# Graph attention on one core: one edge column of every group fetched by one-hot products, in batches of three groups

## The reference

```python
nf = relu(layernorm(x)); ef = edge_attr
for l in range(3):
    f = leaky_relu((nf @ W_ni)[src] + (nf @ W_nj)[dst] + ef @ W_fij + bias, 0.2)
    e = einsum('ehd,hd->eh', f.reshape(-1, 4, 32), attn)
    a = softmax of e over the edges of one dst
    h = segment_sum((nf @ W_node)[src] * a, dst)
    nf, ef = h.mean(heads), f.mean(heads)
return x + nf
```

## Time and profile before

| | |
|---|---|
| median of 3 runs | 3000.43 us (3000.24 to 3002.9) |
| span of the profiled execution | 3006.7 us |
| mean granted PE clock | 0.843 of full speed |
| busy share of the span | DVE 83%, PE 80%, POOL 68%, PEld 62%, ACT 48% |

### The profile page before, as it was taken

How to read it: one execution, slowest core, us unless ns; L and a number is a source line. 1 busy time by engine, 2 the same in 40 slices (tenths; PEclk the granted TensorE clock), 3 DMA queues, 4 the chain that set the end, 5 groups by cost and what they waited for, 6 DMA issues and landing times.

```text
span 3006.7 us, 50077 instructions
## 1 busy us (share of the span) xinstructions
PE 2404.8 (80%) x15871; PEld 1878.0 (62%) x16027; DVE 2490.5 (83%) x6428; ACT 1447.6 (48%) x3416; POOL 2058.9 (68%) x2167
## 2 busy tenths in 40 slices
PE   3388888888887378888888887649999888998984
PEld 1366667676764356667766665337777777776753
DVE  7399999999997468998999998637888888879784
ACT  0155555555555135555556555414445454445452
POOL 6777777777770577777777776377776666667653
PEclk9699988888899589987999999857778787778796
DMA  6235454535342324343435342332333343333222
GB/s 252 64 96 156 122 147 116 152 110 158 110 128 85 112 74 142 119 149 110 157 111 158 110 153 98 118 103 67 100 120 99 98 136 98 108 108 100 91 92 81
DMA packets 139275, 353.92 MB, mean 118 GB/s; under 512 B 43895, under 2 KB 96027, under 8 KB 120207
## 3 DMA queue, kind: packets, MB, share of 16 engines
q1 hardware_dynamic: 67216, 296.09, 27.9%
q0 software_dynamic: 68960, 39.71, 8.6%
q10 hardware_dynamic: 2838, 14.91, 1.3%
HBM read 137.79 MB, written 212.77 MB: 117 GB/s over the span
## 4 chain that ended last, share of the span: by engine, by line
PE 39%; DVE 29%; issue 14%; ACT 9%; POOL 5%; DMA 3%; SPq 1%; DVEq 0%; ACTq 0%; POOLq 0%
DVE U L1349 12%; PE f_ps L695 12%; PE pick_ps L664 10%; PE f_ps L704 9%; PE xT_ps L685 5%; DVE rows L1266 4%; DVE lr L1277 4%; DVE U L1334 3%; POOL rows L554 2%; ACT f_low L850 2%; ACT xT L841 2%; ACT up L901 2%; PE f_ps L714 2%; ACT wide_ps L889 1%; DVE rows L1378 1%
## 5 line engine op out<-in xcount | busy, mean ns | idle before, releaser
L554 POOL DMA_INDIRECT rows<-nf_tab,src_sb x1995 | 1889.3, 947 | 706.9 <-issue 574.9
L704 PEld LDWEIGHTS f_ps<-w_out,lr 128*128 128x128 f32 x4836 | 701.0, 210 | 379.0 <-issue 277.3
L664 PE MATMUL pick_ps<-nf_part,z 125*128 125x160 bf16 x6345 | 630.0, 264 | 258.4 <-issue 217.0
L1349 DVE TENSOR_TENSOR_SCAN U<-wide_ps,U 128x272 f32<-128x272 f32 (+2 forms) x1272 | 801.6, 694 | 3.2 <-ACT wide_ps L889 2.4
L695 PE MATMUL f_ps<-xT,w_edge 97*128 97x512 f32 x1212 | 753.8, 708 | 22.6 <-ACT ef_new L872 12.0
L664 PEld LDWEIGHTS pick_ps<-nf_part,z 125*128 125x128 bf16 x6345 | 564.6, 112 | 289.8 <-issue 241.3
L704 PE MATMUL f_ps<-w_out,lr 128*128 128x36 f32 (+1 forms) x4836 | 649.8, 274 | 31.2 <-DVE lr L1277 28.8
L1277 DVE TENSOR_TENSOR lr<-f_ps,f_low 128x512 f32<-128x512 f32 x606 | 410.0, 677 | 252.4 <-ACT f_low L850 247.0
L850 ACT ACTIVATE f_low<-f_ps 128x512 f32<-128x512 f32 x606 | 361.0, 596 | 495.9 <-PE f_ps L695 495.9
L685 PE MATMUL xT_ps<-ident,rows 128*97 128x128 f32 x2418 | 431.8, 305 | 76.8 <-issue 37.2
L841 ACT ACTIVATE xT<-xT_ps 97x512 f32<-97x512 f32 x606 | 358.8, 592 | 147.8 <-PE xT_ps L685 145.6
(11 more groups left out here) (163 smaller groups left out, 1070.5 us busy)
## 6 DMA issues: line engine op xcount, KB each, us to landing
u_tab<-up SPq DMA_DIRECT2D x144, 1088.0 KB
s_nd<-edge_first SPq DMA_DIRECT2D x48, 768.0 KB
rows<-nf_tab,src_sb POOLq DMA_INDIRECT x1995, 2.5
ef_tab<-ef_new SPq DMA_DIRECT2D x32, 768.0 KB
ef_st<-ef_tab SPq DMA_DIRECT2D x32, 768.0 KB
z<-fifth_tab SPq DMA_DIRECT2D x141, 96.0 KB
edge_first<-s_nd ACTq DMA_DIRECT2D x16, 768.0 KB
ef_st<-in_edge_attr_dram SPq DMA_DIRECT2D x16, 672.0 KB
```

The source lines that it names most:

```text
L554: eng.indirect_dma_start(rows[q % RING][:, c * K:c * K + D], None, nf_tab[:, :], bass.IndirectOffsetOnAxis(ap=src_sb[:, t:t + 1], axis=0)) ...
L664: mm = eng.matmul(pick_ps[:, i * PB:(i + 1) * PB], hot[m % 2][0:NQ, f * PW + i * P:f * PW + (i + 1) * P], nf_part[a][0:NQ, f * PB:(f + 1) ...
L704: mm = eng.matmul(f_ps[n % 2][:, u * m:(u + 1) * m], lr[y][:, u * P:(u + 1) * P], w_out[l][:, 0:m], start=True, stop=True)
L1349: last = eng.tensor_tensor_scan(uh[:, c0 * w:c1 * w], dbc[h % 2][:, 0:(c1 - c0) * w], uh[:, c0 * w:c1 * w], 0.0, ALU.mult, ALU.add)
```

## The change

Every group now has a picked column (groups 0 to 182 of a layer, 61 batches instead of 47), and a batch is three consecutive groups, not three out of four. PE picks in every iteration g up to 173, column i = g % 3 of batch g // 3 + 3, where it ran a filling in every fourth; the fillings stay in iterations 174 to 181. Three batches are picked ahead of the loop, where it was two. DVE's `pick_rows` comes with g % 3 equal to 2 and `make_hot` with g % 3 equal to 0. The first write of `pick_rows` moves to ACT (`take_picks`, at the end of ACT's iteration), and so does the copy of the carry (`carry`, after `take_scores`, ahead of `lay_out`). The two subtractions of `soften` become one instruction over both halves of joined buffers, and `weigh` waits for that one and no longer for the addition behind it. SP loads the index rows by a running count.

```diff
-    NPICK = END // GB + 1
+    NPICK = END // PICK
+    AHEAD = 3
...
         def picks(g):
-            return g % GB < PICK and g // GB < NPICK
+            return g < PICK * NPICK
...
+                    loaded = IDXB + 4
+                    for b in range(IDXB + 2, loaded):
+                        load_fifths(l, b)
...
-                            if b + IDXB + 2 < NPICK:
-                                load_fifths(l, b + IDXB + 2)
+                            while loaded < min(4 * b // PICK + 10, NPICK):
+                                load_fifths(l, loaded)
+                                loaded += 1
...
-                    for b in range(2):
+                    for b in range(AHEAD):
                         for i in range(PICK):
                             pick(b, i)
...
                         turn(g + 2)
-                        b, i = g // GB + 2, g % GB
-                        if g >= 0 and i < PICK and b < NPICK:
+                        b, i = g // PICK + AHEAD, g % PICK
+                        if g >= 0 and b < NPICK:
                             pick(b, i)
                         elif g >= 1:
                             warm(g + 1, FILL_STEADY)
...
                     def weigh(k):
-                        eng.wait_ge(expo_done, k * 3 + 3)
+                        eng.wait_ge(expo_done, k * 2 + 1)
...
+                    def carry(k):
+                        w, before = sub_w(k % NB), sub_w(k % NB - 1)
+                        eng.wait_ge(sums_done, H * k)
+                        eng.activation(carry_of(U[k % 2], w)[:, :, 0, :],
+                                       carry_of(U[1 - k % 2], before)[:, :, before, :],
+                                       ACT.Copy).then_inc(carried, 1)
+
+                    def take_picks(b):
+                        m = l * NPICK + b
+                        q = l * NS + b * PICK // GS
+                        eng.wait_ge(pick_ready, PICK * (m + 1))
+                        if q >= RING:
+                            eng.wait_ge(turned, groups_to(q - RING))
+                            eng.wait_ge(prod_done, subs_to(q - RING))
+                        eng.activation(picked_rows(l, b), pick4[:, :, 0, :], ACT.Copy
+                                       ).then_inc(picked, 1)
...
                         if i == 1 and g >= 2 * GB:
+                            carry(k)
                             lay_out(k - 1)
+                        if g >= 0 and g % PICK == PICK - 1 and g // PICK + AHEAD < NPICK:
+                            take_picks(g // PICK + AHEAD)
...
-                        eng.tensor_tensor(ed3[:, :, 1:w + 1], mx3[:, :, 0:w],
-                                          mx3[:, :, 1:w + 1], ALU.subtract
-                                          ).then_inc(expo_done, 1)
-                        eng.tensor_tensor(e_wt[s][:, 0:w * H].rearrange("p (h t) -> p h t", h=H),
-                                          sc3[:, :, 1:w + 1],
-                                          mx3[:, :, 1:w + 1], ALU.subtract
-                                          ).then_inc(expo_done, 1)
+                        both = [P, 2, H, w]
+                        eng.tensor_tensor(
...
+                            ALU.subtract).then_inc(expo_done, 1)
...
-                            eng.tensor_copy(u4[:, :, 0, :], carry_of(U[1 - s], before)[:, :, before, :]
-                                            ).then_inc(carried, 1)
...
                     def pick_rows(b):
-                        eng.wait_ge(pick_ready, PICK * (m + 1))
...
-                        eng.tensor_copy(to, pick4[:, :, 0, :]).then_inc(picked, 1)
                         for v in range(1, PARTS5):
...
-                        if g >= 0 and i == PICK - 1 and b + 3 < NPICK:
-                            pick_rows(b + 3)
-                        if g >= 0 and i == 0 and b + 4 < NPICK:
-                            make_hot(b + 4)
+                        m = g // PICK + AHEAD
+                        if g >= 0 and g % PICK == PICK - 1 and m < NPICK:
+                            pick_rows(m)
+                        if g >= 0 and g % PICK == 0 and m + 1 < NPICK:
+                            make_hot(m + 1)
```

More of the change, by code:

```diff
@@ L135, in egat_kernel @@
         U = [sb(f"U{s}", [P, CH * W1]) for s in range(2)]
-        mx = [sb(f"mx{s}", [P, H * W1]) for s in range(2)]
+        HW1 = H * W1
+        mx_sc = [sb(f"mx_sc{s}", [P, 2 * HW1 + 2]) for s in range(2)]
+        mx = [a[:, 0:HW1] for a in mx_sc]
+        sc = [a[:, HW1:2 * HW1] for a in mx_sc]
         up = [sb(f"up{s}", [P, SB * UR]) for s in range(2)]
         up3 = [a[:, :].rearrange("p (t c) -> p t c", c=UR) for a in up]
-        sc = [sb(f"sc{s}", [P, H * W1]) for s in range(2)]
-        e_dec = [sb(f"e_dec{s}", [P, H * W1]) for s in range(2)]
-        e_wt = [sb(f"e_wt{s}", [P, H * SB]) for s in range(2)]
+        e_dw = [sb(f"e_dw{s}", [P, 2 * HW1]) for s in range(2)]
+        e_dec = [a[:, 0:HW1] for a in e_dw]
+        e_wt = [a[:, HW1:2 * HW1] for a in e_dw]
         xT = [sb(f"xT{s}", [P, GT * P]) for s in range(2)]
@@ L351, in rows_sem_to, with picked_rows @@
                             if (v % NS) * GS + a < NG)
+        def picked_rows(l, b):
+            s, c = divmod(b * PICK * GT + 2, SUP)
+            return rows3[(l * NS + s) % RING][:, c:c + GT * (PICK - 1) + 1:GT, 0:D]
         def carry_of(u, w):
@@ L678, in turn @@
                         if picks(g):
-                            eng.wait_ge(picked, PARTS5 * (l * NPICK + g // GB + 1))
+                            eng.wait_ge(picked, PARTS5 * (l * NPICK + g // PICK + 1))
                         if n >= 2:
@@ L887, in widen @@
                             eng.wait_ge(sums_done, 4 * k + h - 1)
+                        if h == 0:
+                            eng.wait_ge(expo_done, k * 2 + 2)
                         w, n = sub_w(k % NB) + 1, C - D // 2
@@ L910, in _ @@
                     put_ef(0)
+                    for b in range(AHEAD):
+                        take_picks(b)
                     kl = l * NB - 1
@@ L1015, in _ @@
                     widen(k + 1, 0)
+                    carry(k + 1)
                     lay_out(k)
@@ L1303, in soften @@
                         eng.wait_ge(max_done, k + 1)
-                        eng.tensor_tensor(ed3[:, :, 1:w + 1], mx3[:, :, 0:w],
-                                          mx3[:, :, 1:w + 1], ALU.subtract
-                                          ).then_inc(expo_done, 1)
-                        eng.tensor_tensor(e_wt[s][:, 0:w * H].rearrange("p (h t) -> p h t", h=H),
-                                          sc3[:, :, 1:w + 1],
-                                          mx3[:, :, 1:w + 1], ALU.subtract
-                                          ).then_inc(expo_done, 1)
-                        eng.wait_ge(expo_done, 3 * k + 1)
+                        both = [P, 2, H, w]
+                        eng.tensor_tensor(
+                            e_dw[s][:, :].rearrange("p (a x) -> p a x", a=2)[:, :, 0:n]
+                            .rearrange("p a (h t) -> p a h t", h=H)[:, :, :, 1:w + 1],
+                            mx_sc[s][:, :].rearrange("p (a x) -> p a x", a=2)[:, :, 0:n]
+                            .rearrange("p a (h t) -> p a h t", h=H)[:, :, :, 0:w],
+                            wide(mx[s][:, 0:n].rearrange("p (o h t) -> p o h t", o=1, h=H)
+                                 [:, :, :, 1:w + 1], both),
+                            ALU.subtract).then_inc(expo_done, 1)
+                        eng.wait_ge(expo_done, 2 * k + 1)
                         eng.tensor_tensor(ed3[:, :, 1:w + 1], ed3[:, :, 1:w + 1],
@@ L1387, in _ @@
                     pick_rows(1)
+                    make_hot(3)
+                    pick_rows(2)
                     slice_b(0)
```

30 lines of the change are left out of this document (10 added, 20 removed).

## The result

| | before | after |
|---|---|---|
| median, runs alternating on one chip | 3001.66 us (4 runs) | 3843.66 us (4 runs, 3835.13 to 3868.38) |
| span of the profiled execution | 3006.7 us | 3839.6 us |
| mean granted PE clock | 0.843 | 0.762 |

The ratio is **1.279**, with an interval of 1.273 to 1.285: 842 us slower. The forecast was 700 us slower, 3700 us, and the range ended at 3830. Direction and mechanism came as forecast; the size lies 14 us beyond the range.

A forecast was written before the change was run, and what follows sets the result against it. DVE was taken to bound the kernel at full clock. Twelve groups: 49.1 + 1.3 work + 1.2 first write + 16.3 chains = 67.9 us, +700 us over three loops, so 3700 us; range some 3400 to 3830.

The forecast's parts named there:

- The bound and the chain: DVE bounds at full clock; copies, pick, `edges`, `lower`, `leaky` take 2.87 us, 4.41 at half clock, no longer hidden.
- The stall: DVE idle between `pick_rows` and the next `leaky`: 16.3 us in twelve groups at half clock, 10.2 at full.
- Half clock in every chain: PE waits of some 5 us ahead of a batch's first pick bring half clock to every chain: 16.3 us.
- every second chain: Alternative reading of the clock after PE's waits: only every second chain at half clock, 13.3 us in twelve groups.
- DVE's work: One more batch on DVE, less first writes and carries, with the joined subtraction: +1.3 us in twelve groups.
- The first write behind `widen`: At g % 12 = 8 ACT's first write queues behind `weigh` and two `widen`; DVE idles some 1.2 us.
- What I cost at nothing: Carry on ACT, longer `lay_out` queue, fewer gathers, picks for fillings, index loads, third batch, layer ends: counted as 0.
- an end of +9: End of a layer: taken as 0, with range ends of -4 and +9 us over three layers.
- the third batch ahead of the loop: Some 5 us before the loop, barely covered by DVE's wait for `first`; uncovered, 5 us a layer.
- (a): Rival: chain stays hidden, only added work counts; +20 and +17 us in layers 0 and 1; 3040 us; chance 0.05.
- (b): Rival: faster; a pick every iteration keeps clock at 1.00, chain hidden, layer 2 gains 65 us; some 2938; chance 0.04.
- (c): Rival: half clock throughout, PE the bound at 6.5 us a group; some 4140 us; chance 0.06.

The follow-up runs named there:

- e4: Kernel before, old batches kept, with only the change's small parts: carry and first write on ACT, joined exponents; 2901.22 us, ratio 0.964.
- e7: Kernel before with carry and first write on ACT, joined exponents, plus a second pick buffer and the scan table in SBUF; ratio 0.961.
- e2: The change with picks alternating between two PSUM buffers and the scan table moved to SBUF; 3055.87 us, ratio 1.015.
- e3: The change with 16 fillings on PE ahead of the first pick of every batch; 3534.39 us, ratio 1.176.
- e5: The change with `pick_rows` directly behind `leaky` and ACT's first write behind the scores; 3481.14 us, ratio 1.156.
- e11: The change, one buffer, with the late `widen` behind `lower` and the first write behind the scores on ACT; 3696.19 us, ratio 1.223.
- e8: The change with two pick buffers, scan table in SBUF, late `widen` behind `lower` and first write behind the scores; 2964.34 us, ratio 0.981.
- e6: Kernel before without the steady fillings up to iteration 179; 3015.50 us, ratio 1.0005.
- c2: The change with the scan tables moved to SBUF and still one pick buffer; 3861.96 us, ratio 1.282.

## Why the prediction was right, and where it was wrong

**The bound and the chain: right.** The forecast put the loss into one place, the first pick of a batch ahead of `edges`, in the time between `pick_rows` and the next `leaky`. The second buffer takes 26 of the 28% away, and the pick moved behind `scores` 23. That PE's wait costs nothing in the kernel before holds where the clock is 1.00; in layer 2 it is not quite so, since there the second buffer takes the loop of the old batches from 738.0 to 718.4 us (e4 and e7).

**The stall: right.** The forecast was 16.3 us, all at half clock. Measured in the twelve groups above: 4.54, 3.86, 3.65 and 4.71, or 16.76. PE's waits were to be some 5 us and are 5.17, 5.41, 5.74 and 5.26. Beside the stall of 3.86 us in the timeline above, these are the other three (start, us, engine, line):

```profile
705.36 0.69 DVE L1318 TENSOR_TENSOR lr<-f_ps,f_low 128x512 f32<-128x512 f32 x1 [4.54 <-ACT f_low L861]
...
739.55 0.69 DVE L1318 TENSOR_TENSOR lr<-f_ps,f_low 128x512 f32<-128x512 f32 x1 [3.65 <-ACT f_low L861]
...
757.39 0.69 DVE L1318 TENSOR_TENSOR lr<-f_ps,f_low 128x512 f32<-128x512 f32 x1 [4.71 <-ACT f_low L861]
```

**Half clock in every chain: right.** The clock was 0.50 behind each of the four waits, and 1.00 again ahead of the next. How long it stayed at 0.50 is another matter, below. The section "HAM oscillation" of the page "TensorE: Matmul & The Clock Gate" in the Trainium skill, by which recurring waits bring the clock down at each burst, agrees with that; the other reading, every second chain, is out. The same skill's rule that independent groups of products should rotate through PSUM banks ("Perfetto Trace Analysis", section "Matmuls") is borne out by e2: one buffer 1.279, two 1.015.

**DVE's work: right.** +1.3 us was forecast, 1.23 measured; the joined subtraction takes 0.29 us, the forecast 0.30. **The first write behind `widen`: right,** 1.12 us against 1.2.

**What I cost at nothing: wrong.** This is the step that failed, and the range with it. The sum for twelve groups carried the 1.85 us of idle time over from the kernel before (49.10 less 47.25) and added the chain and the first write alone. Measured, DVE idles 23.19 us: 16.76 in the chains, 1.12 at the first write, **4.46 in three waits that were not in the sum** (1.03, 1.95 and 1.48 us), and 0.85 in small pieces. So 71.68 us in place of 67.9. Of these 3.8 us, 3.5 are the idle time outside the chains and the first write (5.3 in place of the 1.85 carried over); the chains, 0.5 longer than forecast, make most of the rest.

The first and the last of the three have a plain cause, which the code shows: moving `make_hot` and `pick_rows` from g % 4 to g % 3 did not only add a batch, it took away two covers. Before, `make_hot` (1.23 us) stood behind every `soften`, and so lay beside `weigh` and two `widen` on ACT; `pick_rows` (1.1 to 1.4 us) stood behind every pair of heads 0 and 1, and so lay beside the late `widen`. Now, of three sub-batches, one has the step that stood there, one has the other of the two in its place, and one has neither. With g % 12 = 4 nothing but a spread follows `soften`, and DVE waits 1.03 us; with g % 12 = 10 nothing follows the heads, and it waits 1.48. The prediction counted what the moved steps cost, and asked what hides the added ones, but not **what the moved steps had been hiding**. Two kernels bear that out that have ACT's order as in the change and two buffers, and differ only in the batches with their picks and fillings: in e2 the two waits are 1.01 and 1.48 us, and in e7, with the old batches, no wait of DVE between 200 and 700 us of layer 0 is longer than 0.71.

The middle one, 1.95 us, has another cause. It comes where PE is still at half clock a whole group after the third chain, and `edges` takes 1.75 us at 761.03 in place of 1.06. The window from before that chain's pick on, columns as in the twelve groups:

```profile
748.80:762.40 13.60, 9.62 (x46) 7.93 (x47) 6.67 (x16) 5.38 (x12) 4.28 (x6) 0.50 0.08 27
```

The prediction had read from its rows that the clock comes back within one group, and its sum lets half clock cost nothing beyond the `leaky` at the end of the chain. In e3, at a clock of 1.00 behind the same chain (700.8 to 712.2 us), this wait is not there, though ACT's order is the change's and the wait of 1.48 us is; in e5, at 0.50 there (684 to 688 us), it is, with 1.97. In e11 it is gone, and `edges` takes 1.06 us one group after the chain; why the clock comes back sooner there was not settled.

**From twelve groups to the whole.** 3.8 us more in twelve groups would be some 164 us over three loops. The loops are 114 us over the forecast, since the first twelve groups of a layer are cheaper (4.92, 4.92 and 4.68 us a group against 5.97: the first four have no softmax yet), and so are the last six (5.55). The rest of the miss, 19 us, is at the ends: groups 174 to 201 take 4.3, 4.6 and 8.0 us longer, 17 together, where I took 0 with an end of +9; from layer to layer it is 1.9 and 0.6 us more. That the third batch ahead of the loop is nearly covered came true: DVE still waits there, 26.6 us against 39.5.

**The rivals.** (a) and (b), the chain hidden, are out by the 978.1 us of `leaky`. What (b) claimed of the clock, that a pick in every iteration keeps it at 1.00, fell as well: 0.77. Where the chain is out of the way, the change comes out near the 3040 us of (a): e2, at 1.015. That its sum was right does not follow, since the three loops of e2 are 31 and 30 us longer and 31 shorter, where (a) had +20, +17 and nothing. Below the kernel before, as (b) has it, the change's work ends only with ACT's order mended too, in e8. (c), half clock throughout, gave 6.5 us a group and 4140 us; the windows show 1.00 for 10 us behind a stall. The result, 5.97 a group, lies between the forecast and (c), and my range was too narrow because its high end took the loss of the old kernel by layer and no new one: in the changed kernel the three layers no longer differ. That it ended only 14 us short is luck: 119 us of it stood for a loss that did not come.

## What to carry to other kernels

A wait on a buffer is priced by what stands behind it in its engine's queue and by what the bound engine can do meanwhile: against two buffers, the one buffer costs the changed kernel 26% with `edges` queued behind the wait (1.279 and 1.015) and 3% with `edges` ahead of it (1.045), and with the old batches nothing that can be told apart in the whole (0.964 and 0.961). When a step is moved to another phase of the loop, look not only for what will hide it, but for what it was hiding: list the waits of other engines that lay beside it. And take a change apart before judging it: the half of this one that took work off DVE gained 3.6%, and the half that changed the batches hid that under a loss nearly nine times as large.

## What the hardware showed that I had not expected

- Taking 1.0 us of work in twelve groups off DVE, 43 us in all, gained 97 (e4). More than half of that came in layer 2, where the granted clock rose from 0.79 to 0.88; that the clock is the reason is argued, not shown.
- The steady fillings, which keep the clock 0.03 and 0.05 higher in layers 0 and 1, are worth nothing in the whole time: ratio 1.0005 (e6).
- With one long wait in every batch the three layers fall into the same period, 1021 to 1024 us at a clock of 0.77, although they had differed by 68 us before.
- With the scan tables in SBUF, the way from one layer to the next is longer in every kernel that has them there: 100.2 to 102.6 us, against 96.3 to 98.7. In c2 nothing else was changed, so it goes with the tables; why is open.
